# The inverse norms of attention's first tiles on VectorE in place of GpSimd

## The reference, cut to what matters

```
def l2norm(t):
    return t / jnp.clip(jnp.linalg.norm(t, axis=-1, keepdims=True), 1e-12)
...
for l in range(2):
    h = shift_token(x)
    q, k, v = split(h @ wqkv)                  # (tokens, 8 heads, 64) each
    q = l2norm(q) * q_scale;  k = l2norm(k) * k_scale
    q, k = rotary_xpos(q, k)
    o = local_attention(q, k, v)
    x = x + o @ wo
    ... gated MLP ...
```

## Time and profile before

| what | value |
|---|---|
| runs | 558.04, 558.91, 559.72 us, median 558.91 |
| profiled execution | span 556.3 us from its first to its last instruction; no other time of it is on the page |
| PE (TensorE) busy | 488.8 us, 88% |
| DVE (VectorE) busy | 432.2 us, 78% |
| ACT (ScalarE) busy | 348.2 us, 63% |
| POOL (GpSimd) busy | 334.6 us, 60% |
| the power of the norms, L819 | 32 of 2907 ns, 93.0 us in total |
| mean granted TensorE clock | 0.952 |

### The profile page before, as it was taken

The page is one execution under the profiler, slowest core; times in us unless marked ns, Lnnn a source line. Parts: engine busy times, 40 slices in busy tenths (PEclk is TensorE's granted clock), DMA queues, the critical chain, the costliest instruction groups (busy, mean ns, idle before and its releaser), DMA issues.

```text
span 556.3 us, 11701 instructions
## 1 busy us (share of the span) xinstructions
PE 488.8 (88%) x4017; PEld 307.6 (55%) x4017; DVE 432.2 (78%) x1172; ACT 348.2 (63%) x1002; POOL 334.6 (60%) x259
## 2 busy tenths in 40 slices
PE   5650048999999999999989999999999999999997
PEld 3320014467777777543457777777644445667775
DVE  6999999889999886556899999985545688366665
ACT  4971004689999997532579999998647526533332
POOL 5860006999999997776889999995010277420000
PEclk9885559999999999999989999999999999999999
DMA  8400002311111112000041111111000000000000
GB/s 290 165 0 1 1 1 78 69 37 41 39 37 33 39 41 86 2 1 0 2 113 41 40 35 35 41 39 39 1 3 0 0 1 1 1 0 20 20 20 20
DMA packets 14880, 19.93 MB, mean 36 GB/s; under 512 B 2362, under 2 KB 8996, under 8 KB 14692
## 3 DMA queue, kind: packets, MB, share of 16 engines
q1 hardware_dynamic: 14532, 19.08, 12.7%
q10 hardware_dynamic: 288, 0.08, 0.1%
HBM read 8.94 MB, written 1.05 MB: 18 GB/s over the span
## 4 chain that ended last, share of the span: by engine, by line
PE 68%; DVE 14%; POOL 6%; ACT 6%; issue 4%; DMA 1%; DVEq 0%; POOLq 0%; ACTq 0%
PE psT L1396 11%; PE psQK L1469 9%; PE psO L1591 6%; PE psO L1523 5%; PE psQK L1798 5%; PE psS L1571 5%; DVE vst L990 3%; DVE vAB L994 3%; PE psO L1396 3%; PE psS L1870 3%; PE psQK L1605 3%; PE psS L1707 3%; PE psO L1870 2%; PE psQK L1730 2%; PE psO L1709 2%
## 5 line engine op out<-in xcount | busy, mean ns | idle before, releaser
L526 ACT ACTIVATE prob<-psS,nmx 128x128 f32<-128x128 f32 x256 | 89.9, 377 | 18.0 <-DVE nmx L1135 18.0
L819 POOL TENSOR_TENSOR rn<-ssq,half 128x16 f32<-128x16 f32 x32 | 93.0, 2907 | 8.0 <-DVE ssq L1121 7.9
L811 POOL TENSOR_TENSOR ra<-ra,rb 128x512 f32<-128x512 f32 x64 | 80.9, 1284 | 1.0 <-DVE rb L1103 0.9
L666 POOL TENSOR_TENSOR rst<-mv,half 128x4 f32<-128x4 f32 x24 | 25.7, 1070 | 73.8 <-DVE mv L922 63.6
L1469 PE MATMUL psQK<-wqkv,hsA 128*128 128x512 f32 x128 | 62.0, 604 | 1.0 <-DVE hsA L1084 0.6
L526 ACT ACTIVATION_READ_ACCUMULATOR prob<-psS,nmx 128x1 f32 x256 | 55.6, 217 | 0.0
L1100 DVE TENSOR_TENSOR ra<-psQK,rope 128x512 f32<-128x512 f32 x64 | 43.9, 686 | 10.2 <-PE psQK L1469 9.7
L827 POOL TENSOR_TENSOR qkn<-ra,rn 128x512 f32<-128x512 f32 x32 | 49.0, 1532 | 2.5
L1103 DVE TENSOR_TENSOR rb<-psQK,rope 128x512 f32<-128x512 f32 x64 | 43.6, 681 | 0.0
L647 ACT ACTIVATE gel<-psQK 128x512 f32<-128x512 f32 x32 | 19.1, 597 | 37.5 <-PE psQK L1798 37.5
L1114 DVE TENSOR_REDUCE ssq<-sq 128x8 f32<-128x512 f32 x64 | 41.1, 677 | 1.6 <-ACT sq L466 1.3
(11 more groups left out here) (240 smaller groups left out, 1204.1 us busy)
## 6 DMA issues: line engine op xcount, KB each, us to landing
vAB<-vAB SPq DMA_DIRECT2D x62, 128.0 KB, 2.2
wqkv<-in_wqkv SPq DMA_DIRECT2D x2, 768.0 KB, 8.4
big<-in_x SPq DMA_DIRECT2D x4, 256.0 KB, 4.5
ropeb<-in_rope SPq DMA_DIRECT2D x1, 1024.0 KB, 6.5
big<-in_ew SPq DMA_DIRECT2D x2, 512.0 KB, 4.7
wmod<-in_wmod SPq DMA_DIRECT2D x2, 384.0 KB, 6.0
out<-big SPq DMA_DIRECT2D x3, 256.0 KB, 2.3
w<-in_w SPq DMA_DIRECT2D x2, 341.0 KB
```

The lines of the kernel that those rows point to most:

```text
L526: act.activation(prob[:, k, :], psS[:, hb, c * P:(c + 1) * P], ACT.Exp, bias=nmx[:, k:k + 1], accum_out=sums[:, n % 2, k:k + 1]).then_inc( ...
L811: pool.tensor_tensor(o, o, rb[:, r], ALU.add).then_inc(s["sum_" + name], 1)
L819: pool.tensor_tensor(rn[:, :], ssq[:, :], half[:, :], ALU.pow).then_inc(s["rn_ready"], 1)
```

## The change

For tiles 0, 1, 2, 17 and 18 GpSimd's `norms` returns at once. VectorE computes the same inverse square roots directly behind the clamp: a first guess by integer arithmetic on the bits of the float, then two polynomial steps. It takes eight instructions on 128x16, and each waits for the one before (`own.one` adds a semaphore and a wait). The waits that `norms` had, for both users of the old `rn`, are now VectorE's. The last instruction gives the semaphore `rn_ready`, for which the scaled keys and the scaled q wait.

```diff
+EARLY_NORMS = (0, 1, 2, 17, 18)
+SEED = 0x5F3759DF
...
+        rsq = sb("rsq", [P, 16])
...
             def norms(n):
+                if n in EARLY_NORMS:
+                    return
                 pool.wait_ge(s["ssq_max"], n + 1)
...
                 dve.tensor_scalar(ssq[:, :], ssq[:, :], 1e-24, None, ALU.max).then_inc(s["ssq_max"], 1)
+                if n in EARLY_NORMS:
+                    early_norms(n)
+
+            def early_norms(n):
+                dve.wait_ge(s["ssq_max"], n + 1)
+                if n:
+                    dve.wait_ge(s["k_ready"], n)
+                    dve.wait_ge(s["q_ready"], n)
+                own.one(dve.tensor_scalar(rn[:, :].bitcast(I32), ssq[:, :].bitcast(I32), -0.5, float(SEED), ALU.mult, ALU.add))
+                own.one(dve.tensor_tensor(rsq[:, :], rn[:, :], rn[:, :], ALU.mult))
+                own.one(dve.tensor_tensor(rsq[:, :], rsq[:, :], ssq[:, :], ALU.mult))
+                own.one(dve.scalar_tensor_tensor(out=rsq[:, :], in0=rsq[:, :], scalar=-10.0 / 3, in1=rsq[:, :], op0=ALU.add, op1=ALU.mult))
+                own.one(dve.scalar_tensor_tensor(out=rn[:, :], in0=rsq[:, :], scalar=5.0, in1=rn[:, :], op0=ALU.add, op1=ALU.mult))
+                own.one(dve.tensor_tensor(rsq[:, :], rn[:, :], rn[:, :], ALU.mult))
+                own.one(dve.scalar_tensor_tensor(out=rsq[:, :], in0=rsq[:, :], scalar=-0.5 * 0.375 ** 3, in1=ssq[:, :], op0=ALU.mult, op1=ALU.mult))
+                dve.scalar_tensor_tensor(out=rn[:, :], in0=rsq[:, :], scalar=1.5 * 0.375, in1=rn[:, :],
+                                         op0=ALU.add, op1=ALU.mult).then_inc(s["rn_ready"], 1)
```

## The result

The changed kernel took 561.46 us (median of 4 runs, 561.41 to 562.32) against 559.32 us for the kernel before (4 runs, 558.04 to 559.85). The ratio is 1.0058, with a 95% interval of 1.0042 to 1.0074: slower by 3.2 us (2.3 to 4.1). This ratio is not that of the two medians, which alone differ by 2.1 us (1.0038). The median falls on the forecast 561.5, but the forecast built on a loss of 2.6 us; the ratio and the trace say a bit more.

The account below looks back on a forecast made before the run. VectorE and GpSimd were taken as nearly equally late in each layer's start-up. Losses of 1.4 us (layer 0) and 1.2 (layer 1) made 2.6, added to 558.9 for 561.5 us; 80% range 558.4 to 563.3.

Parts of the forecast that it names:

- Where the change can act: Only the start-up before TensorE's steady loop in each layer; norms are hidden in the loop, its period stays 7.25 us.
- (b): Distance from layer 0's first output transposes to tile 17's clamp, 156.97 us before; the forecast had the steady loop unaffected.
- Cost of the chain: VectorE behind each early clamp: eight dependent steps of 0.20 us, 5.0 us new work in layer 0, 3.4 in layer 1.
- Given back in layer 0: VectorE waits and stretched instructions from tile 0's clamp to its scaled output, filled by the new work: 3.6 us.
- the square of tile 2: Layer 0, VectorE's sum of squares waiting for ScalarE's square: spacing from 2.0 to about 1.05, gain 0.95 us.
- The residual wait behind GpSimd: Layer 0, scaled q of tiles 0 and 2 meeting a GpSimd rope sum: a remaining wait of about 0.2 us.
- the stretched clamp of tile 2: Layer 0, clamp held behind a rope sum, read as ending 0.5 us before the rope products: gain 0.45 us.
- Layer 1: From tile 17's clamp: 3.4 us new work, 2.1 given back; the steady loop starts 1.2 us later.
- The locks: Layer 1, two scaled q of 1.56 and 1.49 us held behind GpSimd's scaled keys: gains 0.7 and 0.6 us.
- Clock: Layer 1, TensorE's half-clock stretch hides behind VectorE; rival, chance 13%: it lasts longer, 0.7 to 1.7 us visible.
- GpSimd alone as the bound: Rival for both start-ups: VectorE has room, each early tile gains 1.3 us, 552.4 us in all; chance 14%.
- The collision: Rival: each early chain meets a GpSimd rope sum of 1.25 us, 6.3 us more, 567.8 us; chance 5%.

Follow-up runs that it names:

- e6: Changed kernel plus eight constant TensorE multiplications in layer 1's idle ahead of tile 17's transposes; 562.20 us, ratio 1.0075 to the kernel before.
- e1: Kernel before with VectorE making the norms of tiles 0, 1, 2 only, layer 1 unchanged; 559.44 us, ratio 1.0022.
- e4: Kernel before with VectorE making the norms of tile 1 only; 559.46 us, ratio 1.0021.
- e8: Changed kernel without the second polynomial step, five chain instructions in place of eight, coarse norms; 559.85 us, ratio 1.0033 to the kernel before.
- e3: Changed kernel with one copy of the sums in place of each eight-instruction chain, output false; 555.83 us, ratio 0.9958 to the kernel before.
- e7: Changed kernel with the eight instructions issued in pairs behind four rope products or maxima; 563.35 us, ratio 1.0095 to the kernel before.
- e5: Kernel before plus eight constant TensorE multiplications in layer 1's idle ahead of tile 17's transposes; 557.59 us, ratio 0.9995.
- e9: Kernel before plus eight constant TensorE multiplications in layer 1, with VectorE adding the rope sums of q for tiles 1 and 2; 558.45 us, ratio 1.0004.

## Why the prediction was right, and which terms were off

The mechanism was the forecast one, and the loss was forecast somewhat low. That the median fell on 561.5 is luck. The forecast added 2.6 us of loss and 2.6 us for the distance between the span of a profiled execution and the median of the runs. The distances give a loss of 3.3, and the time of the profiled execution of the changed kernel lies 1.8 above its span (562.32 against 560.5). The two errors nearly cancel.

- *Where the change can act.* Right: (b) is unchanged and the steady period too; GpSimd's 15.0 us less (14.5 forecast) did not make up for the chains.
- *Cost of the chain.* 1.71 (tile 0) and 1.78 forecast from clamp to next instruction, 1.77 to 1.79 measured in layer 0, 0.21 per step for 0.20. New work 5.0 in layer 0, as forecast.
- *Given back in layer 0.* 3.6 forecast, 5.0 - 1.58 = 3.4 measured. The clamp of tile 1 came 6.24 us after that of tile 0 (6.3 forecast), unstretched; that of tile 2 14.54 after (14.1). The mis-sized term is the square of tile 2: the two sums of squares are 1.5 us apart, from 2.0, so 0.5 was returned and not 0.95. The residual wait behind GpSimd was 0.1 at the scaled q of tiles 0 and 2 and not 0.2, which makes up a part. One reading was wrong without harm: before the change the stretched clamp of tile 2 (`112.63 0.67 DVE L1121 TENSOR_SCALAR ssq<-ssq 128x16 f32<-128x16 f32 x1`) does not end 0.5 ahead of the rope products at 113.21. It starts 0.58 ahead of them, where an undisturbed clamp starts 0.11 ahead, and 0.47 came back for the 0.45 forecast.
- *Layer 1.* 1.2 forecast, 1.69 measured. The locks gave back 0.79 and 0.69 as worked out. Missed were the wait for the square of tile 18 (0.37, which puts the clamp 1.83 after the first sum of squares and not 1.54, so 0.29 more; the replay looked for such a wait in layer 0 only) and the idle of 0.29 of unknown cause.
- *Clock.* It was forecast that the slow stretch hides behind VectorE in the changed kernel, and that is shown by e6. Not seen was the other side: in the profiled execution of the kernel before it costs 0.95 us, and e1 and e4, with the same code there, don't have it, so the loss depends on the baseline's clock: 1.7 or 2.6 us for layer 1. Only one execution of the kernel before was traced, so how often it falls there is not shown.
- *Rivals.* GpSimd alone as the bound is refuted by e1, which is slower and not faster, and by e8, in which a chain instruction costs 0.14 us in layer 0 and its full 0.21 in layer 1. The collision is real (e4) and absent in the changed kernel. The prediction counts seven of the eight instructions as open to it, those with two SBUF operands; the one that waited in e4 is the eighth, with a single one, as is the clamp. Sum: 1.4 + 1.2 = 2.6 forecast, 1.58 + 1.69 = 3.3 found.
- The Trainium skill, "VectorE: DVE Perf Modes", "Rules for kernel authors", says that the number of chained instructions counts and not their semaphores. The first half is borne out by e3 and e8. The second is not for instructions this small: in the changed kernel an instruction that waits for its predecessor starts 0.21 us after it, the rope product behind the last one, which has nothing left to wait for, 0.10 after it.

## What to carry to other kernels

An engine that ends the chain of waits may be ahead of the next one by very little. Before work is moved to another engine, replay that engine's queue with the work in its place and count what it was waiting for: what it gets more than this is paid in full. A chain of tiny dependent instructions is dear (8 x 0.21 us for 16 columns each), and where instructions of two engines hold each other up, as GpSimd's sums and VectorE's instructions do here, a move also changes who meets whom, so half a move can be worse in ways that the whole is not (e4), and a later but cheaper chain can be worse than an early one (e7).

## What the hardware showed that was not expected

- An idle of TensorE of 1.88 us was followed by the lower clock in one execution and not in another (kernel before against e1), with the same work around it; likewise 2.0 us of idle at 27 to 29 us (1.00 before, 0.50 in the changed kernel's profile). In these two places it made 0.95 and 0.96 us, nearly a third of the effect under study. It does not always show: in e5 the clock stood at 0.50 at 30 to 31 us too, but the two multiplications ahead, from 28.95 on, took only 1.25 us, and the clamp of tile 0 came at 99.01.
- GpSimd's products and sums hold up a VectorE instruction with two SBUF operands until they end (1.75 us for 0.69, e7), and also one with a single SBUF operand: the clamp and the first guess took 0.87 and 1.20 us for 0.17 (e4). Its power did not: in e9 a sum on VectorE, started inside a power of 2.91 us, took its usual 0.69. VectorE, then GpSimd:

```profile
102.57 0.69 DVE L1112 TENSOR_TENSOR ra<-ra,rb 128x512 f32<-128x512 f32 x1
```

```profile
100.20 2.91 POOL L822 TENSOR_TENSOR rn<-ssq,half 128x16 f32<-128x16 f32 x1 [0.27 <-DVE ssq L1127]
```
